# One core, six networks in a row: summary and int8 attention reordered, and a Hadamard split between two engines

## The reference, cut to what matters

```python
# third, its last lines: h is [512, 2048]
hn = rms_norm(h)                       # per token
x = x + hn @ ternary(w_proj).T
# fourth: the summary is one row of 512 per sequence
z = layernorm(x)                       # outer norm
y = z + summary                        # inner norm follows
x = x + (y - mean(y)) / sqrt(var(y) + eps) * gamma + beta
# fifth: 16 query heads of 32, 4 key heads, causal over 64 tokens
fused = int8_linear(layernorm(x), [w_q; w_k; w_v])
q, k = rope(rms_norm(q)) * q_gain, rope(rms_norm(k))
attn = softmax(where(causal, q @ k.T / sqrt(32), min))
x = x + int8_linear(attn @ v, w_o)
# int8_linear: round(x / (absmax/127)) per token, the same per row of w
# sixth
u = fwht(layernorm(x) * SU_ug)         # Hadamard over 512, scaled
h = silu(u @ W_gate.T * s) * (u @ W_up.T * s)
x = x + fwht(h * SU_dp) @ W_down.T * Wscale_dp
```

## Time and profile before

| | |
|---|---|
| median of three runs | 1047.59 us |
| the profiled execution, its own time | 1047.62 us |
| its span, first to last instruction | 1045.8 us |
| mean granted TensorE clock over the span | 0.886 |
| busy: TensorE / VectorE / ACT / POOL | 907.3 / 680.7 / 478.4 / 200.9 us |
| chain of waits: TensorE / VectorE / ACT / POOL | 72% / 12% / 9% / 3% |

### The profile page before, as it was taken

How to read it: one execution, slowest core, us unless ns; L and a number is a source line. 1 busy time by engine, 2 the same in 40 slices (tenths; PEclk the granted TensorE clock), 3 DMA queues, 4 the chain that set the end, 5 groups by cost and what they waited for, 6 DMA issues and landing times.

```text
span 1045.8 us, 13690 instructions
## 1 busy us (share of the span) xinstructions
PE 907.3 (87%) x5149; PEld 699.4 (67%) x5149; DVE 680.7 (65%) x1099; ACT 478.4 (46%) x790; POOL 200.9 (19%) x168
## 2 busy tenths in 40 slices
PE   5887898999899789999999799886348858999997
PEld 4776454677687578888888544454148748988885
DVE  7443674467665599999998778799775543333333
ACT  2354675233465787777875333342213321333331
POOL 2134441000155200000000034562050010011112
PEclk9999997899699889999999999996655755899999
DMA  8720354671133543343330223310600000022101
GB/s 292 268 92 13 130 187 160 238 263 47 51 101 100 167 161 108 117 140 122 121 102 21 99 103 120 140 41 20 247 0 2 1 14 27 21 61 62 61 21 40
DMA packets 44683, 106.66 MB, mean 102 GB/s; under 512 B 6276, under 2 KB 25532, under 8 KB 39502
## 3 DMA queue, kind: packets, MB, share of 16 engines
q1 hardware_dynamic: 43726, 95.22, 27.2%
q0 software_dynamic: 896, 10.62, 2.6%
HBM read 100.58 MB, written 5.24 MB: 101 GB/s over the span
## 4 chain that ended last, share of the span: by engine, by line
PE 72%; DVE 12%; ACT 9%; POOL 3%; issue 2%; DMA 1%; SPq 1%; ACTq 0%; DVEq 0%
PE banks L41 13%; PE banks L42 13%; PE banks L43 13%; PE banks L1932 5%; PE banks L2495 3%; PE banks L2247 2%; PE banks L359 2%; PE banks L1181 2%; POOL w_low L1867 2%; PE banks L1944 2%; PE banks L1212 2%; PE banks L2214 1%; PE banks L1583 1%; ACT wa_cTh L757 1%; PE banks L1773 1%
## 5 line engine op out<-in xcount | busy, mean ns | idle before, releaser
L157 POOL TENSOR_TENSOR w_low<-w_raw,w_high 128x256 fp32r<-128x256 f32 (+2 forms) x44 | 58.2, 1331 | 181.9 <-ACT w_high L153 181.7
L153 ACT CAST w_high<-w_raw 128x1024 fp32r<-128x1024 f32 (+2 forms) x74 | 56.9, 781 | 25.2 <-PE banks L43 19.5
L41 PE MATMUL banks<-da_xT_high,w_high 128*128 128x512 f32 x128 | 52.0, 406 | 1.4 <-DVE da_xT_low L208 1.4
L2363 POOL TENSOR_TENSOR hf_hl<-hf_h,hf_hh 128x512 fp32r<-128x512 f32 x16 | 24.2, 1514 | 149.8 <-ACT hf_hh L2411 114.1
L42 PE MATMUL banks<-hf_xhl,w_high 128*128 128x512 f32 (+2 forms) x136 | 52.5, 386 | 0.0
L41 PE MATMUL banks<-hf_xhh,w_high 128*128 128x512 f32 (+2 forms) x136 | 52.5, 386 | 0.0
L43 PE MATMUL banks<-hf_xhh,w_low 128*128 128x512 f32 (+2 forms) x136 | 51.8, 381 | 0.0
L43 PE MATMUL banks<-da_xT_high,w_low 128*128 128x512 f32 x128 | 50.8, 397 | 0.0
L42 PE MATMUL banks<-da_xT_low,w_high 128*128 128x512 f32 x128 | 50.6, 395 | 0.0
L1932 PE MATMUL banks<-ff_xT_high,tw_guT 128*128 128x512 f16 x128 | 48.5, 379 | 1.4 <-DVE ff_xT_low L208 1.4
L1932 PE MATMUL banks<-ff_xT_low,tw_guT 128*128 128x512 f16 x128 | 48.5, 379 | 0.0
(11 more groups left out here) (412 smaller groups left out, 2726.6 us busy)
## 6 DMA issues: line engine op xcount, KB each, us to landing
cs_rows<-in_ctx SPq DMA_DIRECT2D x24, 1024.0 KB, 5.0
tw_raw<-in_L_ffn_w_gate_up SPq DMA_DIRECT2D x16, 512.0 KB, 4.3
hf_raw<-in_L_ffn_W_up SPq DMA_DIRECT2D x16, 512.0 KB, 3.5
w_raw<-in_L_xattn_W_o SPq DMA_DIRECT2D x8, 512.0 KB
w_raw<-in_L_attn_Wq SPq DMA_DIRECT2D x8, 512.0 KB
w_raw<-in_L_attn_Wk SPq DMA_DIRECT2D x8, 512.0 KB
w_raw<-in_L_attn_Wv SPq DMA_DIRECT2D x8, 512.0 KB
w_raw<-in_L_attn_Wo SPq DMA_DIRECT2D x8, 512.0 KB
```

Of the source, the lines that this page charges most:

```text
L41: nc.tensor.matmul(out, a[0], b[0], start=start, stop=False)
L153: self.nc.scalar.copy(self.wh[k][:, 0:cols], self.raw[k][:, 0:cols]).then_inc(self.split_hi[k], 1)
L157: self.nc.gpsimd.tensor_tensor(self.wl[k][:, 0:cols], self.raw[k][:, 0:cols], self.wh[k][:, 0:cols].bitcast(F32), ALU.subtract).then_inc(s ...
```

## The change

- Ternary network: the sums of squares move into the down loop, after f = 3, the root to ACT at f = 6, and VectorE reads the sums before its last eight Hadamard half steps. The four summary rows are made by TensorE inside the loop, after f = 8, 10, 12 and 14. Statistics of x follow each residual add. POOL clears the first semaphores before the loop, not after it. The stages are no longer closed for every engine by a wait for all four blocks.
- Summary: the outer norm's mean is left out (the inner norm removes it); scale and add are one instruction; the second norm is folded with gamma and the add to x; statistics of the result are taken between. A small class `Roots` does all roots.
- Int8 attention: the subtraction of the large number goes to ACT. The rotation is one product with both tables and two half-width instructions, all on VectorE. Keys are not repeated; scores are 32 products per block of 64 tokens by 64 keys, on 32 rows and 64 columns of the array each. The mask is added by four bf16 products with the identity. Softmax reads the banks directly, for all 128 partitions at once. Probabilities are 64 keys wide with two heads per transpose: 8 transposes, two copies, 32 products with the values of 64x64. Query heads are reordered on the host.
- Last network: the two outer steps of the transform over 512 (between quarters of 128) are additions and subtractions on VectorE, and TensorE does one 128x128 Hadamard product per quarter, for two blocks (256 columns) at once. Blocks 0 and 1 are normalised and mixed inside the attention's order; the first tile's products are split in two halves of 256 tokens. `t` is a buffer of its own.

Core of the diff:

```diff
@@ TernaryFFN.vector
         self.cy.vector(dve)
+        dve.wait_ge(self.ss_done, 1)
+        v.tensor_scalar(self.inv[:, 0, :], c.bank[:, 0, 0:M], 1.0 / F0, BF16_EPS32, ALU.mult, ALU.add).then_inc(self.var, 1)
         for step in range(3 * FT // 2, 2 * FT):
             self.down.vector(dve, ch, step)
         dve.wait_ge(self.down.done, C)
         self.iw.vector(dve, ch)
-        dve.wait_ge(self.ss_done, 1)
-        v.tensor_scalar(self.inv[:, 0, :], c.bank[:, 0, 0:M], 1.0 / F0, BF16_EPS32, ALU.mult, ALU.add).then_inc(self.var, 1)
         dve.wait_ge(self.std, 1)
@@ TernaryFFN.tensor
+    SUM_AT = 3
+    ROWS_AT = {8: 0, 10: 1, 12: 2, 14: 3}
...
             ins.then_inc(self.y_done, 1)
...
+            if f == self.SUM_AT:
+                pe.wait_ge(self.acc_ok, FT)
+                for m in range(M):
+                    ins = nc.tensor.matmul(c.bank[:, 0, m:m + 1], self.acc[:, m * P:(m + 1) * P], self.ones[:, :], start=True, stop=True)
+                ins.then_inc(self.ss_done, 1)
+            if f in self.ROWS_AT:
+                pe.wait_ge(self.var, 1)
+                summary.tensor_row(pe, self.ROWS_AT[f])
@@ SummaryAttention.vector
+            v.scalar_tensor_tensor(y[:, m, :], c.x[:, m, :], rt.inv(m), c.bank[:, m, :], ALU.mult, ALU.add).then_inc(self.y_ok, 1)
...
+            v.scalar_tensor_tensor(y[:, m, :], y[:, m, :], rt.mean(m), self.gb[:, 0, :], ALU.subtract, ALU.mult).then_inc(self.z_ok, 1)
...
+            v.scalar_tensor_tensor(c.x[:, m, :], y[:, m, :], rt.inv(m), c.x[:, m, :], ALU.mult, ALU.add).then_inc(self.x_ok, 1)
@@ Int8Attention.vector
+            v.tensor_tensor(self.ab[:, :, :, :], q.unsqueeze(2).broadcast_to([P, NB, 2, W]), self.rope[:, :, :].unsqueeze(1).broadcast_to([P, NB, 2, W]), ALU.mult).then_inc(self.ab_ok, 1)
+            dve.wait_ge(self.ab_ok, m + 1)
+            half = W // 2
+            v.tensor_tensor(self.rot[:, m, :, 0:half], self.ab[:, :, 0, 0:half], self.ab[:, :, 1, half:], ALU.add).then_inc(self.rot_ok, 1)
+            v.tensor_tensor(self.rot[:, m, :, half:], self.ab[:, :, 0, half:], self.ab[:, :, 1, 0:half], ALU.subtract).then_inc(self.rot_ok, 1)
@@ Int8Attention.tensor
             for g in range(4):
-                for k in range(C):
-                    rows = slice(g * W, (g + 1) * W)
-                    ins = nc.tensor.matmul(c.bank[:, g, k * P:(k + 1) * P], self.qkT[rows, m, k, :], self.qkT[rows, m, C + k, :], start=True, stop=True)
+                nc.tensor.matmul(c.bank[:, g, 0:4 * S], c.identb[:, :], self.mask4[:, :, :].rearrange("p h k -> p (h k)"), start=True, stop=False)
+            for h in range(4):
+                for b in range(2):
+                    for g in range(4):
+                        rows, tokens = slice(g * W, (g + 1) * W), slice(b * S, (b + 1) * S)
+                        at = h * P + b * S
+                        ins = nc.tensor.matmul(c.bank[tokens, g, h * S:(h + 1) * S], self.qkT[rows, m, at:at + S], self.qkT[rows, m, C * P + b * S:C * P + (b + 1) * S],
+                                               start=False, stop=(h == 3))
...
-                        ins = nc.tensor.matmul(c.bank[:, 6 + h // 8, (h % 8) * (W + 1):(h % 8 + 1) * (W + 1)], self.aT[:, 4 * u + k, :], self.v[:, m, k, :], start=True, stop=True)
+                for half in range(2):
+                    for b in range(2):
+                        keys, tokens = slice(half * S, (half + 1) * S), slice(b * S, (b + 1) * S)
+                        ins = nc.tensor.matmul(c.bank[tokens, 6 + half, j * (W + 1):(j + 1) * (W + 1)], self.aT[m % 2][keys, j, tokens], self.v[keys, m, b, j // 2, :], start=True, stop=True)
@@ HadamardFFN
+    def mixed(self, dve, m):
...
+        for k, op in enumerate((ALU.add, ALU.subtract)):
+            v.tensor_tensor(t[:, :, k, :], x[:, :, 0, :], x[:, :, 1, :], op).then_inc(self.mix_ok, 1)
+        dve.wait_ge(self.mix_ok, 2 * m + 2)
+        for k, op in enumerate((ALU.add, ALU.subtract)):
+            v.tensor_tensor(x[:, k, :, :], t[:, 0, :, :], t[:, 1, :, :], op).then_inc(self.x_mixed, 1)
...
-            for j in range(C):
-                for k in range(C):
-                    h = tab.h_m if bin(j & k).count("1") % 2 else tab.h_p
-                    for part in self.xp:
-                        ins = nc.tensor.matmul(c.bank[:, 4 + m, j * P:(j + 1) * P], h[:, :], part[:, k, m * P:(m + 1) * P],
-                                               start=(k == 0 and part is self.xp[0]), stop=(k == C - 1 and part is self.xp[1]))
+    def tensor_transformed(self, pe, p):
...
+        for k in range(C):
+            out = c.bank[:, 2 * p + k // 2, k % 2 * 2 * P:(k % 2 + 1) * 2 * P]
+            nc.tensor.matmul(out, self.tab.h_p[:, :], self.xp[0][p][:, k, :], start=True, stop=False)
+            ins = nc.tensor.matmul(out, self.tab.h_p[:, :], self.xp[1][p][:, k, :], start=False, stop=True)
```

845 lines of the change are left out of this document (496 added, 349 removed).

## The result

The changed kernel takes 981.1 us (median of 4 runs, 978.8 to 982.6) against 1047.1 (1045.1 to 1048.5) for the kernel before: a ratio of 0.937, 95% interval [0.9345, 0.9393]. The forecast was 1004 with a range of 993 to 1019. The direction was right, and the gain of 66 us is half as large again as the 43.5 forecast. The profiled execution took 980.99 us; its span is 979.2.

A forecast was written before the change was run, and what follows sets the result against it. TensorE was taken to hold 72% of the chain of waits, with the changes falling between 667.1 and 905.0 us. Terms 9.5 - 5 - 10.5 - 22.5 - 15 = -43.5 took 1047.6 to 1004, range 993 to 1019.

The forecast's parts named there:

- stage 4: Four attention blocks to the last add, 792.1 to 860.9: smaller products, 46 ns a record, 46 us for 68.8, -22.5.
- stage 3: Last q, k, v row to first transposes of probabilities, 755.4 to 792.1: cheaper rotations, fewer key transposes, -10.5.
- stage 1: Ternary network's down product, 667.1 to 706.8: VectorE idles 9.5 us waiting for the sums, slower by +9.5.
- stage 5: Last add to end of first up and gate products, 860.9 to 905.0: 128 Hadamard products become 16, -15.
- loop: Steady loop of the last network, after 905.0: keeps its instructions, no change forecast.
- Stage 2: First residual add to last q, k, v row, 707.4 to 755.4: shorter chain of adds, statistics and roots, -5.
- Rival C: Down product of the ternary network: VectorE's wait costs nothing, as contention with POOL goes away; 0 there, total 995; 12%.
- A: Attention blocks: half of the small products' loads do not overlap, +14, total 1018; chance 16%.
- B: Attention blocks: a small tile costs as much per record as a full-width one, total 1075, slower; chance 4%.
- D: Some 60 handovers cost 0.15 to 0.2 more, or the loop starts at 1.2 GHz: +10, total 1014; 14%.

The follow-up runs named there:

- late_sum: Changed kernel with VectorE's wait for the mean square's sums moved back behind its last eight Hadamard steps and ACT's root at f = 9: 976.4 us.
- late_split: late_sum with VectorE's wide clip and wide cast of the weights each cut into ten pieces of 512: 974.4 us.
- max_twice: Changed kernel with VectorE taking each block's maximum of the scores twice, the first into a tile nobody reads: 984.8 us.
- hadamard_whole: Changed kernel with the activations' Hadamard transform wholly on TensorE, 64 products of 256 columns for 16, no add and subtract steps on VectorE: 979.9 us.
- values_swapped: Changed kernel with the two inner loops of the value products exchanged, so row halves alternate from product to product: 975.4 us, one run.
- full_width: Changed kernel with score and value products back at full width, 16 of each per block for 32; results not the reference's: 1008.0 us.
- values_twice: Changed kernel with each of the 32 value products of a block issued twice in a row, same operands and output: 987.6 us.
- warm: Changed kernel with products that nobody reads given to TensorE while it waits in stages 3 to 5: 975.3 us.

## Why the prediction was wrong, step by step

The run gained 22.5 us more than forecast. By stage the difference is 10.1 in stage 4, 5.7 in stage 3, 4.9 in stage 1 and 2.7 in stage 5, of which the loop took back 1.7.

- **Stage 1 (+9.5; measured +4.6).** The gap was right, 9.09 us. The terms that failed are those behind it, +3 for steps that now run beside POOL and -3 for those that no longer do. The eight steps took 15.7 for 14.8, +0.9. Out of POOL's way the wide clip and cast took 2.83 each for 3.80 and 3.77 (-1.9), the weights' scalings 6.1 for 7.2 (-1.0), the small scalings 2.0 for 3.0 (-1.0), and the old wait of 1.2 in front of `var` is gone. 9.1 + 0.9 - 1.9 - 1.0 - 1.0 - 1.2 = 4.9. late_sum shows the contention by bringing it back, late_split by taking it away again. Rival C (0) falls, though half of what it said, contention that goes away, is what the forecast missed.
- **Stage 2 (-5; measured -5.1).** Right.
- **Stage 3 (-10.5; measured -16.2, or -15.4 by the marks of the earlier trace rows).** The two score products with their masks were priced at 4.6 each and take about 2.3. The first now ends on TensorE (764.97) before VectorE's third rotation (765.97), so the 1.4 us that it was to stand on the path are gone, and the second gives 2.5; with the 0.7 for handovers, which were not needed, that is 4.6 of the 4.9.
- **Stage 4 (-22.5; measured -32.6).** This is the step that failed most, and its term is the price of a small record. I took 22 ns from L1550 at full clock and made 46 of it, for half clock in the whole stage (twice 22 is 44). The rows after show 18 at full and 30 at half, 14 and 20 for the scores, a mask of half the width, and a clock of 0.69 on average. TensorE's busy time is 23.3, not 36.4. The idle time, forecast at 10, is 12.9, because VectorE leads, which the prediction had ruled out (20.4 of 36.2 us of the chain; max_twice: 3.9 of 4.9 us on the path). One wait in it had no term at all: the root for blocks 0 and 1, moved into the blocks, comes with a table load of 1.28 on ACT (797.85), and VectorE stands 2.32 us for it. I kept 8 us a block for VectorE beside a TensorE time that was 13 too long; with the right one VectorE's 31 of 36 us would have stood out.
- **Stage 5 (-15; measured -17.7).** The size lies in the range, in part by luck, since half of the reason is wrong. At 1.2 GHz 256 columns cost the same 0.21 us that 128 cost in the earlier trace rows, so the wider product makes the stage shorter; what the two halves give was not tested. The stage did not run at 1.2 GHz throughout, as forecast, but at 0.64 on average. That VectorE takes over two of the factors gives nothing that can be read (hadamard_whole).
- **Loop (0; measured +1.7).** Not explained: it lies between 140.8 and 142.9 in all traces.
- **Rivals.** A and B pointed the wrong way: both asked whether a small product could be dearer than 46 ns. values_swapped and the 18 to 30 ns of the rows after show that neither holds. D (dearer handovers) falls as well: no stage came out longer than forecast, only the loop did, by 1.7. None of my cases had a small product cheaper, though the low end of my own bound (23 ns) was the nearer one.

## What to carry to other kernels

A small-tile product read at full clock is not to be doubled for a stage that is only partly at 1.2 GHz (here it took 1.7 times as long at 0.50, the scores 1.4 times): price it from both ends and let the end that lowers the time be a case of its own. When one engine's work in a stage halves, add up the next engine's busy time over the same stage before naming what is idle. Before moving TensorE work to VectorE in a stretch at 1.2 GHz, try leaving it: the work may pay for itself by the clock it brings, as in hadamard_whole, or it may not, as in the kernel before. A wide VectorE instruction beside a POOL step on the path should be moved behind it, or cut if VectorE can bear the price (late_split).

## What the runs showed of the hardware that I had not expected

- Records of 64x64 tiles follow each other at 18 ns at full clock and of 32x64 tiles at 14. Over the whole of stages 3 and 4 they cost 24 and 18 ns, against 197 and 145 for the full-width records of full_width in the same place.
- In three of four doubled runs of 128 small records TensorE paused for 0.7 to 2.1 us, behind 79, 121 and 104 of them, and waited for nothing that the trace shows (values_twice). The fourth run had no pause, and runs of 64 had none.
- POOL and VectorE take turns, whole instruction by whole instruction: two POOL subtractions of 1.3 took 3.9 each, and each ended 1.1 us behind the wide VectorE instruction beside it (late_sum). Cut to 512 columns, VectorE's instructions let them through at 1.5, but VectorE then paid 11.3 for 6.6.
- TensorE was busy for 27.2 us on end with products of 128 columns at a granted clock of 0.50 (before, 869.95 to 897.15); products of 256 columns in the same place had it at 1.00 from 817.8 on, having started at 813.98 (hadamard_whole).
- Idle time of TensorE filled with 92 products of 128 columns that nobody reads raised the granted clock of stage 5 from 0.64 to 0.93 and shortened it by 3.3 of 26.4 us (warm).
